# Three tiles instead of two summed by token on TensorE, with their rounding remainders made on GpSimd

## What is computed

```python
def reference(...):
    x = x + _L0_ffn_ref(_L0_cond_ref(x, ...), L0_ffn_w_gate, L0_ffn_w_up, L0_ffn_w_down)
    x = x + _L1_ffn_ref(_L1_cond_ref(x, ...), L1_ffn_gate_w, L1_ffn_expert_w, L1_ffn_expert_b)
    return x

def _L1_ffn_ref(x, gate_w, expert_w, expert_b):
    logits = xf @ gate_w.T                       # xf: 1024 x 512, 32 experts
    w, idx = jax.lax.top_k(logits, 2)
    w = jax.nn.softmax(w, axis=-1)
    combine = zeros.at[token, idx].add(w)
    out = sum over experts of combine[:, e, None] * (xf @ expert_w[e].T + expert_b[e])
```

## Time and profile before

| | us |
|---|---|
| median of 3 runs (290.9 to 291.02) | 290.93 |
| the profiled execution's own time | 290.29 |
| its span | 288.5 |
| TensorE busy | 268.8 |
| VectorE busy | 139.1 |
| ACT busy | 75.8 |
| POOL busy | 70.3 |

### The profile page before, as it was taken

How to read it: one execution, slowest core, us unless ns; L and a number is a source line. 1 busy time by engine, 2 the same in 40 slices (tenths; PEclk the granted TensorE clock), 3 DMA queues, 4 the chain that set the end, 5 groups by cost and what they waited for, 6 DMA issues and landing times.

```text
span 288.5 us, 4472 instructions
## 1 busy us (share of the span) xinstructions
PE 268.8 (93%) x1592; PEld 162.0 (56%) x1592; DVE 139.1 (48%) x398; ACT 75.8 (26%) x136; POOL 70.3 (24%) x69
## 2 busy tenths in 40 slices
PE   7878999999999999999999999999999999999910
PEld 3345677688877778788877774333333333333700
DVE  3367775776703343477331355414563211332796
ACT  2456654344111133333301112211011111101000
POOL 0522500000000000007332224457544543341000
PEclk9999999999999999999999999999999999999975
DMA  7999700000000100046019999548999999963955
GB/s 266 401 355 340 250 3 0 3 0 2 0 36 36 39 22 15 2 166 272 1 44 413 407 419 422 220 118 305 375 421 419 418 416 414 409 257 100 403 205 199
DMA packets 19382, 61.97 MB, mean 215 GB/s; under 512 B 4420, under 2 KB 6116, under 8 KB 15008
## 3 DMA queue, kind: packets, MB, share of 16 engines
q1 hardware_dynamic: 14208, 51.03, 45.7%
q0 software_dynamic: 3712, 8.09, 7.7%
q10 hardware_dynamic: 1440, 2.56, 2.4%
HBM read 54.89 MB, written 13.99 MB: 239 GB/s over the span
## 4 chain that ended last, share of the span: by engine, by line
PE 86%; DVE 7%; DMA 2%; ACT 2%; issue 1%; SPq 0%; DVEq 0%; ACTq 0%
PE bank L1358 27%; PE bank L1503 26%; PE bank L1539 14%; PE bank L1476 4%; DVE acc L1218 4%; PE bank L1413 3%; DMA xp_first<-in_xp 2%; PE bank L1241 2%; PE bank L1434 2%; DVE acc L1223 2%; PE bank L1420 1%; PE bank L1303 1%; DVE y0lo L892 1%; PE bank L1251 1%; PE bank L1452 1%
## 5 line engine op out<-in xcount | busy, mean ns | idle before, releaser
L1503 PE MATMUL bank<-wbuf,xT 128*64 128x512 f32 (+1 forms) x448 | 77.8, 598 | 0.0
L1539 PE MATMUL bank<-md,hid 128*128 128x512 f32 x176 | 48.3, 415 | 0.0
L631 POOL DMA_INDIRECT slots<-kept,sid x16 | 15.9, 993 | 122.4 <-DVE sid L998 119.4
L1503 PEld LDWEIGHTS bank<-wbuf,xT 128*64 128x64 f32 (+1 forms) x448 | 20.9, 123 | 39.5 <-issue 38.5
L1034 DVE COPY xT<-bank 128x512 f32<-128x512 f32 x21 | 14.5, 691 | 50.7 <-PE bank L1476 50.6
L1539 PEld LDWEIGHTS bank<-md,hid 128*128 128x128 f32 x176 | 31.8, 189 | 8.3 <-issue 2.9
L1358 PE MATMUL bank<-y0hi,mg 128*128 128x512 f32 x88 | 35.3, 412 | 0.6 <-ACT y0hi L703 0.6
L1358 PE MATMUL bank<-y0hi,mu 128*128 128x512 f32 x88 | 33.8, 396 | 0.7 <-DVE mu L896 0.7
L1358 PE MATMUL bank<-y0lo,mg 128*128 128x512 f32 x88 | 33.7, 394 | 0.2 <-DVE y0lo L892 0.2
L1358 PE MATMUL bank<-y0lo,mu 128*128 128x512 f32 x88 | 33.6, 393 | 0.0
L822 ACT ACTIVATE res<-bank,recs 128x512 f32<-128x512 f32 x19 | 13.1, 687 | 66.8 <-PE bank L1503 66.8
(11 more groups left out here) (191 smaller groups left out, 285.5 us busy)
## 6 DMA issues: line engine op xcount, KB each, us to landing
wbuf<-in_w SPq DMA_DIRECT2D x32, 1024.0 KB, 13.9
r_tab<-in_zero SPq DMA_DIRECT2D x1, 4096.0 KB, 25.1
wbuf<-r_tab SPq DMA_DIRECT2D x8, 512.0 KB, 7.9
acc<-in_x SPq DMA_DIRECT2D x1, 2048.0 KB, 15.5
y_tab<-yv SPq DMA_DIRECT2D x8, 256.0 KB, 5.8
out<-acc ACTq DMA_DIRECT2D x8, 256.0 KB, 2.1
base<-in_base SPq DMA_DIRECT2D x3, 352.0 KB, 7.1
xp_first<-in_xp SPq DMA_DIRECT2D x1, 1040.0 KB, 6.9
```

Of the source, the lines that this page charges most:

```text
L631: pool.indirect_dma_start(out=slots, out_offset=bass.IndirectOffsetOnAxis(ap=sid[:, j, k:k + 1], axis=0), in_=rec[:, j, k], in_offset=None ...
L1503: v = mm(RS[t % 2][p0:p0 + w], xT[x_slot(t)][:, c, p0:p0 + w], wbuf[buffer(r)][:, c], start=(c == 0), stop=(c == DC - 1))
L1539: v = mm(DN[j % 2][:], hid[:, t, part, c], md[:, c], start=(c == 0 and part == 0), stop=(c == HC - 1 and part == 1))
```

## The change

`HOT` goes from 2 to 3. Tile 18 is no longer scattered; tiles 18, 19 and 20 are summed by token on TensorE. Their one-hots and rows lie in one more dead weight buffer each, and the parts in later ones. ACT now evicts these tiles to `res` in float32 as it does the others, and copies `res` to the rounded high half in a second instruction; POOL, behind its last scatter, subtracts that from `res` for the remainder. VectorE's `low_part` is gone. TensorE sums tiles 18 and 19 into four banks first, then waits for tile 20's remainder, finishes these four and does the other four. VectorE's hot additions stand one part later, and the last two pairs stand together.

```diff
-HOT = 2
+HOT = 3
...
-HOT_AT, PART_AT, ROWS_AT = DEAD[0], DEAD[1:1 + NT // 2], DEAD[1 + NT // 2]
+HOT_AT, PART_AT, ROWS_AT = DEAD[0:2], DEAD[2:2 + NT // 2], DEAD[2 + NT // 2:4 + NT // 2]
...
@@ POOL
             for t in range(TS - LAG, TD):
                 scatter_tile(t)
+            for i in range(HOT):
+                pool.wait_ge(high_rows, i + 1)
+                nc.gpsimd.tensor_tensor(hot_rows(i, 1), res[(TD + i) % U][:], hot_rows(i, 0).bitcast(F32), ALU.subtract).then_inc(low_rows, 1)
...
@@ ACT
             def evac(n, b, slot, bank_, rows_=P):
                 act.wait_ge(r_mm, n + 1)
-                out = hot_rows(slot - TD, 0) if TD <= slot < TS else res[b][0:rows_]
-                nc.scalar.activation(out, bank_[0:rows_], ACT.Copy, scale=recs[0:rows_, slot, 2:3].bitcast(F32)).then_inc(res_done, 1)
+                nc.scalar.activation(res[b][0:rows_], bank_[0:rows_], ACT.Copy, scale=recs[0:rows_, slot, 2:3].bitcast(F32)).then_inc(res_done, 1)
...
                 evac(t, t % U, t, RS[t % 2], height(t))
+                if t >= TD:
+                    act.wait_ge(res_done, t + 1)
+                    nc.scalar.activation(hot_rows(t - TD, 0), res[t % U][:], ACT.Copy).then_inc(high_rows, 1)
...
@@ VectorE
-            def low_part(i):
-
-                t = TD + i
-                dve.wait_ge(res_done, t + 1)
-                nc.vector.scalar_tensor_tensor(hot_rows(i, 1), RS[t % 2][:], recs[:, t, 2:3].bitcast(F32), hot_rows(i, 0).bitcast(F32),
-                                               ALU.mult, ALU.subtract).then_inc(low_rows, 1)
-
...
-            for i in range(HOT):
-                low_part(i)
...
             for j in range(NT):
                 add_part(j)
-                if j >= TPH:
-                    add_hot(2 * (j - TPH))
-                    add_hot(2 * (j - TPH) + 1)
+                if j >= TPH + 1:
+                    add_hot(2 * (j - TPH - 1))
+                    add_hot(2 * (j - TPH - 1) + 1)
+            add_hot(NT - 2)
+            add_hot(NT - 1)
...
@@ TensorE
             pe.wait_ge(hot_done, HOT)
-            pe.wait_ge(low_rows, 1)
-            for j in range(6):
-                add_up(0, j)
+            pe.wait_ge(low_rows, HOT - 1)
+            for i in range(HOT - 1):
+                for j in range(4):
+                    add_up(i, j)
             pe.wait_ge(low_rows, HOT)
             pe.wait_ge(res_done, bodies * XU + TS)
-            for j in range(6):
-                add_up(1, j)
-            for j in range(6, NT):
-                add_up(0, j)
-                add_up(1, j)
+            for j in range(NT):
+                for i in range(HOT - 1 if j < 4 else 0, HOT):
+                    add_up(i, j)
```

More of the change, by code:

```diff
@@ L173 @@
 DEAD = sorted((b for b in range(NA) if b >= XU), key=lambda b: (LAST_USE[b], b))
-HOT_AT, PART_AT, ROWS_AT = DEAD[0], DEAD[1:1 + NT // 2], DEAD[1 + NT // 2]
-assert max(LAST_USE[b] for b in (*PART_AT, ROWS_AT)) < TD - 1
+HOT_AT, PART_AT, ROWS_AT = DEAD[0:2], DEAD[2:2 + NT // 2], DEAD[2 + NT // 2:4 + NT // 2]
+assert max(LAST_USE[b] for b in PART_AT) < TD and max(LAST_USE[b] for b in ROWS_AT) <= TD
 C_ID = 0
@@ L330, in build_adaln_ffn @@
         res += [ex.put(f"res{U - 1}", [P, D], F32)]
-        rows_split = [[put(f"rows{i}{half}", [P, D], F32R, WB_AT[ROWS_AT] + (2 * i + half) * D * 4) for half in range(2)] for i in range(HOT)]
-        hot = [put(f"hot{i}", [P, TOK // E, E], F32R, WB_AT[HOT_AT] + i * TOK * 4) for i in range(HOT)]
+        rows_split = [[put(f"rows{i}{half}", [P, D], F32R, WB_AT[ROWS_AT[i // 2]] + (2 * (i % 2) + half) * D * 4) for half in range(2)] for i in range(HOT)]
+        hot = [put(f"hot{i}", [P, TOK // E, E], F32R, WB_AT[HOT_AT[i // 2]] + i % 2 * TOK * 4) for i in range(HOT)]
         cf = own("cf", [P, CF_W], F32)
@@ L429, in build_adaln_ffn @@
         zero_in, hot_done, hot_mm = sem("zero_in"), sem("hot_done"), sem("hot_mm")
-        low_rows = sem("low_rows")
+        high_rows, low_rows = sem("high_rows"), sem("low_rows")
         def tiles_of(flat):
@@ L597, in _ @@
                         r = sp.value_load(todo[0:1, bass.ds(g * XU + (u + 2 * XMAX - XU), 1)], min_val=0, max_val=E - 1)
-                        sp.wait_ge(res_out[u], g * 16 + 16 * (len(range(u, TS, U)) - 1))
+                        sp.wait_ge(res_out[u], g * 16 + 16 * (len(range(u, TD, U)) - 1))
                         load_further(r, c, u)
@@ L834, in _ @@
             with act.If(bodies > 0):
+                act.wait_ge(low_rows, HOT)
                 with act.Fori(1, bodies + 1) as g:
@@ L837, in _ @@
                         act.wait_ge(further_in[u], g * 16)
-                        act.wait_ge(res_out[u], g * 16 + 16 * (len(range(u, TS, U)) - 1))
+                        act.wait_ge(res_out[u], g * 16 + 16 * (len(range(u, TD, U)) - 1))
                         evac(g * XU + (TS + u - XU), u, TS + u, RS[(TS + u) % 2])
@@ L1051, in one_hot @@
                 dve.wait_ge(landed, count)
-                dve.wait_ge(r_mm, LAST_USE[HOT_AT] + 1)
+                dve.wait_ge(r_mm, LAST_USE[HOT_AT[i // 2]] + 1)
                 tok = recs[:, t, 3:4].bitcast(F32)
```

1 line of the change is left out of this document (removed).

## The result

The changed kernel took 288.58 us, the median of 4 runs (288.05 to 288.94); the kernel before took 290.95 us beside it. The ratio is 0.9917, 95% interval 0.990 to 0.9934: faster by 2.4 us, where 288.5 was predicted. The number is right, but two of its steps were not, and their errors nearly cancel. The profiled execution took 288.05 us, its span is 286.2 us.

The account below looks back on a forecast made before the run. VectorE's additions and the loads of the parts were taken to bound the tail. 2.75 - 0.2 - 0.1 = 2.45 us off the 290.93 us median gave 288.5 us, range 286.9 to 290.1.

Parts of the forecast that it names:

- Steps 1 and 2: Last scatter becomes tile 17's, its issue lengthened 0.94 us by the third one-hot; loads of the parts start 2.05 us earlier.
- Step 3: VectorE's additions of parts begin at 265.55, wait 1.0 us for part 2, and end 2.75 us earlier.
- the first rival: The third part is not late, so additions run without waiting from 265.6: 3.8 us less, 287.4; chance 14%.
- Step 6: POOL's subtractions collide with VectorE's additions of parts: 0.2 us taken, bounds 0 and 1.2 us.
- the second case: VectorE subtraction L957, two SBUF inputs, ran within a POOL compare at 0.69 us, no longer than with POOL idle.
- The second rival: POOL and VectorE lock each other out; tile 20's subtraction holds VectorE 1.2 us: 1.45 us less, 289.5; chance 20%.
- Steps 4, 5 and 7: POOL's subtraction takes 1.2 us; TensorE's 48 sums end at 278.7, hidden under VectorE; the last four stores cost 0.1 us.
- The slower rival: POOL is starved between additions of parts, so TensorE starts its sums late and binds: 292.5 us or worse; chance 10%.
- the prediction's own far end: Tile 20's full 1.2 us hold on VectorE, plus the last landing delayed by its whole 0.94 us: 290.2; 6 points.

Follow-up runs that it names:

- the second trace of the kernel before: The kernel before, unchanged, traced again on a chip where it took 290.79 us: ratio 1.0.
- the two slower chips: Chips that ran the first eight follow-up kernels, the changed kernel again (ratio 0.9912) among them; the kernel before took 298.20 and 297.84 us there.
- the last kernel above: Changed kernel with remainders on VectorE (tile 19's behind part 1, tile 20's behind part 3) and the third one-hot behind the last xT copy: 287.80 us, ratio 0.9908.
- the first trace of the kernel before: The kernel before, unchanged, as profiled for the prediction: that execution took 290.29 us.
- the third experiment: Changed kernel with POOL writing zeros (memset) in place of the remainders of tiles 19 and 20, left out of the sums: ratio 0.9863.

## Why the prediction came out right

The steps in its order, against the first sum by token as zero:

| step | predicted | measured |
|---|---|---|
| 1, 2: loads earlier by | 2.05 | 6.37 - 3.33 = 3.04 |
| 3: first addition earlier by | 3.87 | 4.79 |
| 3: wait for part 2 | 1.0 | none |
| 6: POOL beside the additions costs | 0.2 | 1.93 |
| 7: stores cost | 0.1 | 2.72 - 2.59 = 0.13 |

**Steps 1 and 2.** The scatter was lengthened by the one-hot as predicted. Its landing came 3.8 us after its issue and not the 4.5 + 0.2 taken. The 4.5 us of the earlier trace rows was one landing behind the last weights; the second trace of the kernel before has 3.7. I had taken one sample of a quantity that scatters by most of a microsecond. Counted from the end of its issue, the last scatter landed 1.6 us later in all eight traces of the two slower chips; there the landing followed the issue. In the other five traces tile 17's landed 1.9 to 3.5 us later, so there the issue alone does not set it, as predicted. But in the trace of the result it is 1.9, only 0.3 more than on idle engines: the lengthened issue had nearly caught up with the weights, and taking it away brought the 0.4 us above.

**Step 3 failed in its bound.** "The loads are the next bound" did not come true; what came true is the first rival, given 14%. A cause can be named now. One queue's row (packets, MB, share of the 16 DMA engines) in the 2 us from 268 of before and in the 2 us from 269 of after reads:

```profile
q8 instruction: 1, 0.02, 3.1%
```

```profile
q8 instruction: 1, 0.02, 3.4%
```

It is a fetch of 16 KB of code at about 269.5 in both traces. Its one packet took 3.1% and 3.4% of 16 engines for 2 us, that is one DMA engine for 1.0 and 1.1 us. The parts behind it came late. In the changed kernel part 4 (issued 263.2) landed 8.4 us after its issue; in the last kernel above, whose fetch met part 5, part 4 took 6.9:

```profile
DMA to landing us min/median/max: 8.4/8.4/8.4
```

```profile
DMA to landing us min/median/max: 6.9/6.9/6.9
```

In each of the 13 traces such a fetch stands among the loads, and from one part on they are late by about 1 to 1.5 us; which one, part 2 to 6, goes by when the fetch came. In the first trace of the kernel before it is part 2, in the second (fetch at 270.6) part 3. No run took the fetch away, so the cause rests on this coincidence; and why the delay can be 1.5 us where the fetch took 1.1 is open. The prediction said that it saw no cause for the late part; this row was there to be read.

The loads were closer to binding than the missing wait says. Part 4 landed at 263.2 + 8.4 = 271.6 and its first addition began at 272.81. Without the 1.93 us that POOL cost it would have come to it at 270.88 and waited about 0.7 us (an estimate from this trace; with the zeros of the third experiment the wait was 0.40).

**Step 6 failed in its size:** "I take 0.2, since the second case is the nearer one". The nearer row was not L957 beside a compare with one input but the scatter beside the one-hot. Each subtraction holds one addition for 0.96 to 0.98 us, once for 1.14: 12 meetings in the six traces where POOL subtracts beside the additions. The second rival had the mechanism and 1.2 us, but for tile 20 alone; I had thought tile 19's would be taken out of the wait for part 2, which did not exist. The Trainium skill ("SBUF — State Buffer", who interferes with whom) states the rule that the runs bear out for two inputs: the memset, which reads nothing, cost nothing, and the subtraction held the next addition. That the second is blocked until the first ends, as the prediction put it, the traces nearly bear out: POOL waits for the running addition, and in all 12 meetings the held addition ends 0.55 to 0.57 us behind the end of POOL's subtraction. An addition takes 0.69, so it is let go 0.12 to 0.14 us before POOL is through. The 1.14 us is the one time when POOL began between two additions. For one input the traces do not agree: the multiplication held VectorE for 0.29 us and not for its length.

**Steps 4, 5 and 7 held.** POOL's subtraction is 1.27 us (1.2 taken), the 48 sums 11.14 us (11.3), without a wait, and the stores cost 0.13. The slower rival did not occur: POOL got in between two additions that lay 0.02 us apart in all 12 meetings, behind the one that was running or in the gap itself, so it was not starved here.

Together: 4.79 - 1.93 - 0.13 = 2.73 us; this execution's first sum came 0.43 us later than in the first trace of before, which leaves the 2.3 us between the spans. The forecast summed 2.75 - 0.2 - 0.1. Two errors, 2.0 us in favour and 1.7 against, made the number nearly exact. That is luck, though the two are tied: with POOL's 1.93 us gone, about 0.7 of it would have come back as a wait for part 4. The range, with both rivals inside it, earned its keep more than the value did. Its upper bound is 0.1 us short of the prediction's own far end (a gain of 0.7, 290.2), which changes nothing.

## What to carry to other kernels

Work moved from VectorE to GpSimd beside VectorE instructions with two SBUF inputs can cost VectorE more than it saves: here 0.96 us for each 128x512 f32 subtraction, where making it on VectorE costs 0.6. In the traces that is clear, in the time it was too small to tell. Before pricing a landing by one row, look for what else was on its DMA engines, code fetches included, and whether that will meet the same transfer once it moves. And where a tail is bound by one engine behind one transfer, ask for the last producer of that transfer: here it was one scatter fewer that gave the time. The remainders' move alone gave none that could be told (0.9998), the third tile without it 0.9900.

## What the runs showed of the hardware

- A GpSimd subtraction (two SBUF inputs) that begins during a VectorE addition waits for its end and then holds the next addition for 0.96 to 0.98 us, until 0.12 to 0.14 us before its own end. Once it began between two additions and held the next for 1.14 us. A multiplication with one SBUF input held it for 0.29 us, a memset not at all.
- An indirect DMA's issue on GpSimd beside the VectorE comparison of the one-hot took 1.92 instead of 0.98 us in every trace, and moving the comparison away gave the 0.94 us back to the issue each time. The landing got all of it where it came 1.6 us behind the end of the issue, and 0.4 us where weights were still on the DMA engines.
- One code fetch of 16 KB among the loads took one of the 16 DMA engines for 1.0 to 1.1 us, and from one part on the loads landed about 1 to 1.5 us later, in all 13 traces; no run was without it.
